# A mixture-of-experts tower on Trainium2: the centring of the expert sums moved from their turn into the weights

## The reference, cut to what matters

```
h = patches(x) @ W.T + b
h = h + rnn(layernorm(h))
h = h + moe_layernorm(layernorm(h))

def moe_layernorm(x, gate_w, gate_b, w1, b1, w2, b2, gamma, beta):   # 16 experts, top 2, D=64, F=128
    gate_logits = x @ gate_w + gate_b
    topk_w = softmax of the two highest logits
    expert_out = relu(x @ w1 + b1) @ w2 + b2          # for every expert
    y = x + sum over the two chosen of topk_w * expert_out
    mu, var = mean(y), var(y)                          # over the 64 features
    return (y - mu) / sqrt(var + EPS) * gamma + beta
```

## Time and profile before

| what | value |
|---|---|
| device time, median of 3 runs | 536.03 us (535.11 to 537.37) |
| the profiled execution: its own time | 535.65 us |
| the profiled execution: span from first to last instruction | 533.9 us |
| TensorE matmul busy | 507.5 us, 95% of the span |
| VectorE busy | 418.0 us, 78% |
| ScalarE busy | 350.3 us, 66% |
| GpSimd busy | 173.6 us, 33% |
| mean granted clock of TensorE, share of 2.4 GHz | 0.989 |

### The profile page before, as it was taken

The page is one execution under the profiler, slowest core; times in us unless marked ns, Lnnn a source line. Parts: engine busy times, 40 slices in busy tenths (PEclk is TensorE's granted clock), DMA queues, the critical chain, the costliest instruction groups (busy, mean ns, idle before and its releaser), DMA issues.

```text
span 533.9 us, 8845 instructions
## 1 busy us (share of the span) xinstructions
PE 507.5 (95%) x3044; PEld 338.5 (63%) x3044; DVE 418.0 (78%) x841; ACT 350.3 (66%) x606; POOL 173.6 (33%) x126
## 2 busy tenths in 40 slices
PE   4777999999999999999999999999999999999992
PEld 4454667676766766666676666667676766666652
DVE  1545797896969788796969889696988879797665
ACT  3545575857768586766858675776858577666661
POOL 4220111613424252432335162332426244222223
PEclk9997999999999999999999999999999999999998
DMA  6219175855829194573909476482928456483901
GB/s 142 67 40 221 40 170 130 189 124 121 175 70 229 40 208 102 125 182 93 211 25 206 104 171 144 103 192 63 219 59 187 109 129 151 110 189 77 205 19 30
DMA packets 29755, 69.04 MB, mean 129 GB/s; under 512 B 6432, under 2 KB 8464, under 8 KB 29584
## 3 DMA queue, kind: packets, MB, share of 16 engines
q1 hardware_dynamic: 29712, 68.49, 56.2%
HBM read 60.39 MB, written 8.08 MB: 128 GB/s over the span
## 4 chain that ended last, share of the span: by engine, by line
PE 89%; issue 3%; POOL 2%; DMA 2%; DVE 1%; ACT 1%; POOLq 0%; SPq 0%; DVEq 0%; ACTq 0%
PE pZ L845 37%; PE pO L858 34%; PE pA L871 4%; PE pA L760 3%; PE pA L796 2%; PE pA L814 2%; PE pB L760 2%; PE pA L784 2%; PE pB L826 1%; POOL inv_std L348 1%; DMA spread<-gates_dram 1%; PE pB L814 1%; PE pA L772 1%; PE pA L785 1%; DMA gates_dram<-gt 1%
## 5 line engine op out<-in xcount | busy, mean ns | idle before, releaser
L478 ACT ACTIVATE hexp<-pZ,b1c 128x784 f32<-128x784 f32 x256 | 223.1, 911 | 107.2 <-PE pZ L845 107.1
L858 PE MATMUL pO<-hexp,w2s 128*64 128x392 f32 x1024 | 199.8, 506 | 0.6 <-ACT hexp L478 0.3
L845 PE MATMUL pZ<-xt,w1hi 128*128 128x392 f32 x512 | 189.2, 369 | 1.4 <-ACT xt L405 1.0
L637 DVE SCALAR_TENSOR_TENSOR prod<-pO,b2c,spread 128x392 f32<-128x392 f32 x256 | 149.0, 620 | 42.3 <-PE pO L858 38.6
L845 PE MATMUL pZ<-xt,w1lo 128*128 128x392 f32 x512 | 175.4, 343 | 0.0
L348 POOL TENSOR_TENSOR inv_std<-var,nhalf 112x7 f32<-112x7 f32 x48 | 75.8, 1580 | 198.0 <-DVE var L546 198.0
L845 PEld LDWEIGHTS pZ<-xt,w1hi 128*128 128x128 f32 x512 | 97.2, 190 | 48.1 <-issue 28.7
L858 PEld LDWEIGHTS pO<-hexp,w2s 128*64 128x64 f32 x1024 | 70.3, 136 | 75.9 <-issue 63.1
L653 DVE TENSOR_TENSOR acc<-acc,prod 128x784 f32<-128x784 f32 x111 | 111.3, 1003 | 0.1
L845 PEld LDWEIGHTS pZ<-xt,w1lo 128*128 128x128 f32 x512 | 97.4, 190 | 0.0
L546 DVE TENSOR_REDUCE var<-sq 112x7 f32<-112x455 f32 x48 | 29.9, 624 | 49.2 <-ACT sq L409 36.4
(11 more groups left out here) (95 smaller groups left out, 472.7 us busy)
## 6 DMA issues: line engine op xcount, KB each, us to landing
spread<-gates_dram SPq DMA_DIRECT2D x128, 392.0 KB, 9.0
h_dram<-h SPq DMA_DIRECT2D x16, 248.1 KB, 2.4
h2c<-h_dram SPq DMA_DIRECT2D x16, 248.1 KB, 7.2
xcur<-x_in SPq DMA_DIRECT2D x16, 196.0 KB, 7.2
out<-yo SPq DMA_DIRECT2D x15, 196.0 KB, 7.0
w1f<-w SPq DMA_DIRECT2D x2, 512.0 KB, 5.9
w2s<-w SPq DMA_DIRECT2D x1, 512.0 KB, 3.7
gates_dram<-gt SPq DMA_DIRECT2D x16, 28.0 KB, 2.0
```

The costliest lines, as they stand in the source:

```text
L478: nc.scalar.activation(hexp[u % RING][:, :].rearrange("p (b c) -> p b c", b=2), halves(pZ[u % 2]), ACT.Relu, bias=b1c[:, u:u + 1]).then_in ...
L637: nc.vector.scalar_tensor_tensor(out=prod[q % RING][:, b * HALF:(b + 1) * HALF], in0=halves(pO)[:, b, :], scalar=b2c[:, q:q + 1], in1=spre ...
L845: last = nc.tensor.matmul(halves(pZ[e % 2])[:, b, :], w[:, e, :], xt[par][:, b * HALF:(b + 1) * HALF], start=(k == 0), stop=(k == 1))
L858: last = nc.tensor.matmul(halves(pO)[k * D:(k + 1) * D, b, :], w2s[:, e, :], hexp[e % RING][:, b * HALF:(b + 1) * HALF], start=True, stop= ...
```

## The change

What it does, part by part:

- w2 and b2 have their mean over the 64 output features taken out once, in the fill. For w2, VectorE sums each expert's row of 64 (a reduction of 128x1024 to 128x16) after the low parts of w1, and later subtracts a 64th of the sum in place (one pass over 128x1024) after the first gates. For b2, TensorE multiplies the loaded `b2f` with `fold` into `pO` (two small matmuls) ahead of the first `x2_turn`, and ScalarE copies it to `b2c`. Four semaphores guard this. The first `product` and the first `second_layer` wait for it.
- `sum_turn` becomes seven plain transposes (the transpose form of the matmul, against the 128x128 identity) into two banks: four tiles of 128 columns into `pA`, three into `pB`. As `pB` is used, it waits for the copy "gt" of the next step's gates out of `pB`, and for "h2" in every step that has it, in place of the wait for the copies of the embedding.
- `close_center` moves from ScalarE to VectorE and becomes two reductions, one for each bank, that add the two halves of every tile's 128 columns (innermost stride 64) into `cen`: 112x512 to 112x256 and 112x384 to 112x192. In VectorE's slot 12 it stands where `norm_var` stood. `norm_var` comes after the `product` of slot 13.
- the chain `CLOSE` has one stage more.

```diff
-        CLOSE = Chain("close_stage", "turned center square var rstd norm gamma out")
+        CLOSE = Chain("close_stage", "turned center_a center square var rstd norm gamma out")
...
-            def close_center(s):
-                CLOSE.wait(act, s, "turned")
-                nc.scalar.activation(cen[:, :, :], tiles_of(pA), ACT.Copy).then_inc(CLOSE.sem, 1)
-
...
-                    if close and u == 12:
-                        close_center(t - 1)
+                    if close and u == 13:
                         square(CLOSE, t - 1, "center", 2, cen[:, :, :])
...
             high_part(0)
+            act.wait_ge(b2_turned, 1)
+            nc.scalar.activation(b2c[:, :], pO[:, 0:Q], ACT.Copy).then_inc(b2_centred, 1)
             keep_h1(2, 0)
...
+            def close_center(s):
+                CLOSE.wait(dve, s, "turned")
+                for bank, some, n in ((pA, slice(0, PAIRS), PAIRS), (pB, slice(PAIRS, TILES), TILES - PAIRS)):
+                    nc.vector.tensor_reduce(cen[:, some, :], bank[0:P, 0:n * 2 * D].rearrange("p (i k d) -> p i d k", k=2, d=D),
+                                            X, ALU.add).then_inc(CLOSE.sem, 1)
...
+                if known(n, 1):
+                    dve.wait_ge(b2_centred, 1)
...
                             product(t - 1, Q - 1, 1 - par)
+                    if close and u == 13:
+                        norm_var(CLOSE, c, 2)
+                    if experts and u % 2 == 1:
                         if u > 3:
                             add(t, u // 2 - 2, par)
...
                     if close and u == 12:
-                        norm_var(CLOSE, c, 2)
+                        close_center(c)
...
             w1_low_part(1)
+            dve.wait_ge(experts_loaded, EXPERTS_LOADED)
+            nc.vector.tensor_reduce(w2sum[:, :], w2s[:, :, :], X, ALU.add).then_inc(w2_summed, 1)
             add_state(0, 0)
...
             gate_weights(0)
+            dve.wait_ge(w2_summed, 1)
+            nc.vector.scalar_tensor_tensor(out=w2s[:, :, :], in0=w2sum[:, :].unsqueeze(2).to_broadcast([F, E, D]),
+                                           scalar=-1.0 / D, in1=w2s[:, :, :], op0=ALU.mult, op1=ALU.add)\
+                .then_inc(w2_centred, 1)
             add_state(1, 1)
...
+                if known(n, 1):
+                    pe.wait_ge(w2_centred, 1)
+                    pe.wait_ge(b2_centred, 1)
...
-            def sum_turn(s, par, embed=False, mix=False):
+            def sum_turn(s, par, gate=False, mix=False):
                 pe.wait_ge(summed, s * Q + Q)
-                if embed:
-                    pe.wait_ge(h1_kept, 2 * (s + 4) + 2)
-                elif mix:
+                if gate:
+                    GATE.wait(pe, s + 2, "gt")
+                if mix:
                     STATE.wait(pe, s + 3, "h2")
                 if not known(s, 1):
                     CLOSE.wait(pe, s - 1, "out")
-                for i in range(TILES):
-                    last = nc.tensor.matmul(tiles_of(pA)[:, i, :], acc[par][:, i * P:(i + 1) * P], fold[:, 0:D],
-                                            start=True, stop=True)
+                for bank, first, end in ((pA, 0, PAIRS), (pB, PAIRS, TILES)):
+                    for i in range(first, end):
+                        last = nc.tensor.transpose(bank[0:P, (i - first) * 2 * D:(i - first + 1) * 2 * D],
+                                                   acc[par][:, i * P:(i + 1) * P], ident[:, :])
                 last.then_inc(CLOSE.sem, 1)
...
             embed_in(2)
+            pe.wait_ge(experts_loaded, EXPERTS_LOADED)
+            for k in range(2):
+                rows = slice(k * D, (k + 1) * D)
+                last = nc.tensor.matmul(pO[rows, 0:Q], fold[rows, 0:D], b2f[rows, :], start=True, stop=True)
+            last.then_inc(b2_turned, 1)
             x2_turn(0)
```

More of the change, by code:

```diff
@@ L79, in vit_tower_kernel @@
         w2s = sb("w2s", [F, E, D])
+        w2sum = sb("w2sum", [F, E])
+        b2f = sb("b2f", [2 * D, Q])
         b2c = sb("b2c", [2 * D, Q])
@@ L170, in vit_tower_kernel @@
         spread_in = [sem(f"spread_loaded_{i}") for i in range(PARTS)]
+        w2_summed = sem("w2_summed")
+        w2_centred = sem("w2_centred")
+        b2_turned = sem("b2_centred_by_pe")
+        b2_centred = sem("b2_centred")
         z_ready = sem("z_ready")
@@ L229, in vit_tower_kernel @@
                       (gbias[:, :], gate_b.partition_broadcast(P))]
-        expert_loads = [(b1c[:, :], b1), (w2s[:, :, :], w2), (b2c[:, :], b2),
+        expert_loads = [(b1c[:, :], b1), (w2s[:, :, :], w2), (b2f[:, :], b2),
                          (gam[:, :], gamma.partition_broadcast(P)), (bet[:, :], beta.partition_broadcast(P))]
@@ L910, in body @@
                     if close and u == 11:
-                        sum_turn(t - 1, 1 - par, embed, mix)
+                        sum_turn(t - 1, 1 - par, gate, mix)
                     if gate and not known(t, 1) and u == 1:
```

## The result

The changed kernel takes 523.95 us (median of 4 runs, 523.67 to 524.21) against 535.57 us before (median of 4, 534.93 to 537.37): a ratio of 0.978, 95% interval 0.977 to 0.980. That is 11.6 us faster, where 9.8 were forecast. The time lies 0.25 us under the low end of the range. The mechanism came as forecast; a second, smaller gain at the end of the program was not in the sum. A repeat in a later group of runs (e5) gave 524.28 us against 534.91, ratio 0.980 (0.979 to 0.982).

What follows compares the result with a forecast made beforehand. TensorE, busy 95% of the span, was taken as the bound: 0.65 us a step over fifteen calls gives 9.8 us, fill nothing, so 535.65 becomes 525.9, and 526.2 with the median 0.4 above the profile. Range 524.2 to 530.8 us.

Steps and rivals of the forecast that it cites:

- What bounds, and the turn: TensorE bounds the end; in each step, transposes of 0.75 us replace matmuls of 1.40, gaining 0.65.
- The close on VectorE: The two new reductions take about 1.2 us a step, fit VectorE's 2.22 us gap and do not delay TensorE.
- C: Time of both close reductions on VectorE, about 1.2 us; also a rival: many reduction results cost extra, 547 us, chance 0.05.
- The threshold of 1.7 us: Time of VectorE's two close reductions from which TensorE starts to wait; the whole gain is gone at 2.36 us.
- the tightest place: Pair 2's second layer on TensorE, which needs the first half of pair 1's product, with 0.14 us to spare.
- The fill: New work on w2 and b2 fits idle time in the fill and costs nothing; without that cover 2.9 us at most.
- rival D: TensorE's clock falls in each step because transposes replace matmuls, a net loss of 0.85 us a step: 549 us, chance 0.04.
- The step that failed: The last step's close stays as before and moves with TensorE, give or take 0.5 us.
- the low end of 524.2: Bottom of the range: the all-bounds gain of 11.1 us from 536.0, and 0.7 more for scatter of the runs.
- A: Rival: VectorE's two close reductions take 1.7 to 2.3 us, so TensorE waits; 3.8 us of gain left, 532.2 us, chance 0.09.
- B: Rival: the transposes cost like two passes, 1.40 us a step, or miss TensorE's path; nothing won, 536 us, chance 0.06.

Runs made afterwards that it cites:

- e5: The changed kernel run once more, unaltered, in a later group beside the kernel before: 524.28 us against 534.91, ratio 0.980.
- e8: The changed kernel with the seven turns written as plain fp32 matmuls against the identity instead of transposes: 536.30 us, against 534.91 for the kernel before.
- e1: The kernel before with only the change's fill added (w2 and b2 centred once), its turn, close and order kept: 535.55 us against 536.02.
- e11: The changed kernel with each of VectorE's two close reductions done a second time into an unread tile: 530.92 us, ratio 0.991 to the kernel before.
- e2: The changed kernel without the fill's centring of w2 and b2, so its output lacks part of the mean's removal: 523.88 us against 536.02 before.
- e3: The kernel before with GpSimd's multiplication by gamma of step 14 held until VectorE's add of pair 6 in the last step: 534.83 us against 536.02.
- e12: The changed kernel with the close's norm_var put back ahead of pair 5's product, right behind the reductions: 529.66 us, ratio 0.989 to the kernel before.
- e4: The changed kernel with GpSimd's multiplication by gamma of step 14 held until VectorE's add of pair 6 in the last step: 524.26 us.
- e6: The changed kernel with TensorE's sum turn moved behind the first layer of slot 12: 523.75 us, ratio 0.981 to the kernel before.
- e7: The changed kernel with twelve extra matmuls, results unread, in TensorE's stop in the fill: 522.40 us, ratio 0.9765 to the kernel before.
- e10: The changed kernel with twelve extra matmuls in the fill, run again beside the kernel before with them: 522.15 us, ratio 0.975 to the kernel before.
- e9: The kernel before with twelve extra matmuls in TensorE's stop in the fill: 533.08 us, ratio 0.996 to the kernel before.

## Why the prediction was right or wrong

**What bounds, and the turn: right.** TensorE bound the end; 15 turns gave 9.8 us, as computed. They took 0.71 us, between the 0.66 and 0.75 of the bounds, and 0.06 us of waiting for "gt" came on top, where I took nothing and allowed up to 0.15. That the sum of 0.65 a step was hit to the hundredth is luck: these two small misses cancel. That it was the transpose form, and neither the number of columns nor the move of the centring by itself, e8 and e1 show.

**The close on VectorE: right in time, order and slack.** C was 1.15 us; the stride cost nothing. The threshold of 1.7 us stood up to e11. Wrong was the tightest place: I looked for the smallest margin of a second layer against its product and did not check the turn of x2 against the low part, whose margin is the same.

**The fill: right.** Its work was free (e1, e2). The clock in the fill, which cost 1.3 to 1.6 us for each 3.4 us at half, was no term of the sum; I had its row (0.54 from 44 to 50 us) and used it for rival D alone.

**The step that failed** is the last sentence of the fill's part, "the last step's close is as before; it moves with TensorE, give or take 0.5", and with it the low end of 524.2, which held only the cheapest transposes and 0.7 for scatter. The code of the last close is as before, but what goes on beside it is not. The new slot order shifted GpSimd's gamma of the step before behind VectorE's last add, which had waited 0.73 us for it, and TensorE's wait ahead of the last turn fell from 1.63 to 0.89 us. That is 0.8 us in both profiles (e3: 0.79 alone, from this order alone). The wait in its old length was also followed by a fall of the clock in two of four profiles, for up to 1.5 us more (e1, e12). The slow add stood in the trace of the kernel before: 1.72 us at 521.40, where adds take 0.96 as a rule. I took the tail as a thing that shifts as a whole.

From the forecast of 526.2 to the measured 523.95 it is 2.25 us. The tail is 0.79 of it. Another 0.46 is the yardstick: the kernel before had a median of 536.03 in the three runs that I had and 535.57 with the fourth. The rest, 1.0 us, is about the 0.91 us ahead of the first turn, clock and scatter. The time lies 0.25 us outside the range, and each of the three is larger than that: without any one of them it would have been inside. The tail is the one that an experiment pins down.

**The comparison's footing.** The unchanged kernel scattered over 2.6 us in e1's group (534.3 to 536.9) and over 2.0 in e5's, the changed one over 0.5 and 1.5, and its variants e4 and e6 over 1.9 and 3.0. That the change also makes the time steadier isn't shown. With the extra matmuls the changed kernel scattered over 1.3 and 1.1 us (e7, e10), the one before still over 3.2 (e9). The lead is 11.6 us by the medians of the result, 10.6 in e5's group and 10.9 between e9 and e10, and steps and tail make 10.6. The median of the kernel before alone was 536.02, 534.91 and 535.44 in three groups on three chips. What the last half to one microsecond is, the tail's clock in unprofiled runs or the chip, stays open.

**Rivals.** A, B and C did not come; e8 shows B's price to be real for the plain form, e11 shows A's threshold. D did not come either: the granted clock stayed at 1.00 in all steady steps of the changed kernel. It fell where TensorE stood still. The Trainium skill (TensorE: Matmul & The Clock Gate, Part 4) states that transposes don't count as busy for the gate as matmuls do. A step's transposes, with matmuls around them, cost no clock here.

## What to carry to other kernels

An fp32 matmul by a constant that folds, centres or adds cost two instructions for each tile here (14 for seven tiles, 1.40 us); where the constant can be folded into weights once, a transpose of half the price (0.71 us) does the rest, and another engine with a gap adds the halves. Put the new work of that engine exactly into its gap, and what waits for a third engine behind the work that doesn't: the same instructions in the old order gave back half of the gain (e12). Count the tail's rows by themselves, since small shifts between engines there change who waits for whom.

## What was not expected of the hardware

- A stop of TensorE of 2.3 to 2.9 us in the fill was followed by 3.4 us of half clock in ten profiles and by 6.8 in one (before). Each 3.4 us cost 1.3 to 1.6 us of time. Twelve idle matmuls in the stop took 1.9 us off the time; the same three lines took 2.4 us off the kernel before (535.44 to 533.08). In the tail, a wait of 1.63 us was followed by half clock in two profiles (e1, e12) and by none in two (before, e9), and a wait of 0.89 us in none.
- The head of a series of matmuls costs about 0.1 us (0.26 to 0.29 to the second one, 0.18 between the others), so splitting the series in two cost as much here as the wait of 0.06 us that it removed (e6).
- A VectorE add of 0.96 us stretched to 1.72 when GpSimd's multiplication had begun ahead of it, while a GpSimd power of 1.49 us stretched to 2.15 beside VectorE's add (changed kernel, 507.23).
